# A head's TensorE order rearranged: scores, prediction and xs product together, output rows ahead of w_x, squares last, tile 3 in tile 2's bank

## The reference, cut to what matters

```python
# keys, values, queries of a head; chunk_loss = sum(mean((mlp(k) - v)**2) * lr)
grads = vmap(grad(chunk_loss))(mem_ws, keys, lr, values)     # for w0 and w1, by chunk
momentum = assoc_scan(mom_gate, -grads); updates = assoc_scan(1 - decay, momentum)
x    = einsum('bhncd,bhnde->bhnce', q, mem_w0 + updates[0])
vals = einsum('bhncd,bhnde->bhnce', silu(x), mem_w1 + updates[1])
vals = rmsnorm(vals) * (gamma + 1) * gate
out  = concat_heads(vals) @ w_combine
```

## Time and profile before

| | |
|---|---|
| median of 3 runs | 1191.07 us (1189.88 to 1191.84) |
| profiled execution | 1189.44 us, its span 1187.6 us |
| PE busy | 1100.7 us, 93% of the span |
| PE weight loads busy | 917.9 us, 77% |
| DVE, ACT, POOL busy | 720.1, 679.8, 561.9 us (61%, 57%, 47%) |
| mean granted TensorE clock | 0.965 |

### The profile page before, as it was taken

One profiled execution on the slowest core, in us unless ns is written; L12 is line 12 of the kernel. 1 busy time (PEld: TensorE's weight loads), 2 busy tenths in 40 slices (PEclk: granted clock), 3 DMA queues, 4 the chain that ended last, 5 costly groups with the idle time before them and its releaser, 6 DMA issues. The chain is left out here.

```text
span 1187.6 us, 20255 instructions
## 1 busy us (share of the span) xinstructions
PE 1100.7 (93%) x6649; PEld 917.9 (77%) x6650; DVE 720.1 (61%) x1892; ACT 679.8 (57%) x1369; POOL 561.9 (47%) x571
## 2 busy tenths in 40 slices
PE   4589869999999999999999899998999899999995
PEld 3356547788888888888888788887888788888884
DVE  4488856877655655655555455554555555556785
ACT  4666635566565565655555455554556455556663
POOL 3167753487764434444433343343434343344553
PEclk9888959999999999999999899999999999999998
DMA  9133330000300000000000000000000000002222
GB/s 209 38 89 90 89 115 1 1 21 21 98 24 1 2 16 10 10 10 18 9 10 7 20 8 10 8 9 19 8 8 9 19 8 10 3 5 77 88 88 72
DMA packets 57537, 40.32 MB, mean 34 GB/s; under 512 B 4595, under 2 KB 52061, under 8 KB 57310
## 3 DMA queue, kind: packets, MB, share of 16 engines
q1 hardware_dynamic: 53894, 32.10, 9.9%
q0 software_dynamic: 2304, 4.74, 1.2%
q10 hardware_dynamic: 1248, 2.23, 0.6%
HBM read 21.71 MB, written 15.50 MB: 31 GB/s over the span
## 5 line engine op out<-in xcount | busy, mean ns | idle before, releaser
L1105 DVE TENSOR_TENSOR p_sb<-bank,cf 128x512 f32<-128x512 f32 (+3 forms) x512 | 218.9, 483 | 1.1 <-PE bank L828 1.0
L1286 POOL TENSOR_TENSOR sq_rest<-sq,sq_high 128x450 f32<-128x450 f32 x64 | 67.2, 1050 | 247.1 <-ACT sq_high L995 247.1
L851 PE MATMUL bank<-p_sb,du_t 128*128 128x450 f32 (+3 forms) x512 | 131.1, 399 | 0.0
L851 PE MATMUL bank<-p_sb,err_t 128*128 128x450 f32 (+3 forms) x512 | 130.1, 397 | 0.0
L851 PEld LDWEIGHTS bank<-p_sb,err_t 128*128 128x128 f32 x512 | 85.0, 190 | 40.0 <-DVE p_sb L1105 16.9
L851 PEld LDWEIGHTS bank<-p_sb,du_t 128*128 128x128 f32 x512 | 82.0, 190 | 43.8 <-issue 29.8
L1138 DVE SCALAR_TENSOR_TENSOR acc<-bank,rg,acc 128x128 f32<-128x128 f32 x224 | 62.9, 344 | 84.6 <-POOL rg L1274 84.6
L1290 POOL TENSOR_TENSOR sq_low<-sq_rest,sq_mid 128x450 bf16<-128x450 f32 x64 | 66.6, 1041 | 100.1 <-ACT sq_mid L1012 99.9
L973 ACT ACTIVATE s_sb<-bank 128x512 f32<-128x512 f32 x64 | 38.3, 599 | 108.0 <-PE bank L828 108.0
L967 ACT ACTIVATE xs<-bank 128x450 f32<-128x450 f32 x64 | 35.1, 548 | 109.7 <-PE bank L851 108.5
L1174 DVE SCALAR_TENSOR_TENSOR du<-q_sb,bank 128x512 f32<-128x512 f32 x64 | 44.0, 688 | 87.5 <-PE bank L828 87.5
(11 more groups left out here) (304 smaller groups left out, 3193.0 us busy)
## 6 DMA issues: line engine op xcount, KB each, us to landing
x<-in_L_attn_inputs SPq DMA_DIRECT2D x16, 256.0 KB, 3.1
rows<-sorted_rows SPq DMA_DIRECT2D x40, 64.5 KB, 1.8
sorted_rows<-xl_all SPq DMA_DIRECT2D x1, 2064.0 KB, 14.7
x_rows<-x SPq DMA_DIRECT2D x8, 256.0 KB, 2.4
xn_rows<-xn SPq DMA_DIRECT2D x8, 256.0 KB, 2.4
xl_all<-xl SPq DMA_DIRECT2D x8, 256.0 KB, 3.4
ew<-in_L_ffn_w SPq DMA_DIRECT2D x8, 256.0 KB, 4.2
attn_out<-acc SPq DMA_DIRECT2D x7, 256.0 KB, 2.0
```

What stands on the lines that cost most here:

```text
L851: last = pe.matmul(out[:, P * i:QW], rows[:, i, :], p_sb[:, P_COL[i]:P_COL[i] + QW - P * i], start=False, stop=True, skip_group_check=True)
L1105: last = nc.vector.tensor_tensor(dst, src, w, ALU.mult)
L1286: nc.gpsimd.tensor_tensor(sq_rest[:], sq[:], sq_3[0][:], ALU.subtract).then_inc(g_rest, 1)
```

## The change: what it does

On PE the scores for s are parted: the tiles in halves (`NEAR`, 0 and 1) stay where they were, and the f32 ones (`FAR`, 2 and 3) come after the prediction and the xs product. Then follow the block's transpose (now into QA), the transposes of `err`, and only then the application to `err_t`. The scores for f are made in one go ahead of the transposes of `du`. The second expert layer and the output rows come ahead of the product with `w_x` and its application; the squares come last. Tile 3 lies in bank 6 beside tile 2. ACT makes `err_t` directly after `vals`, ahead of the squares. DVE weighs the near tiles, makes the first `q_sb`, and then weighs the far ones; the block's first DVE operation comes after the second `q_sb`.

The diff, cut to its core:

```diff
-SC_BANK = [4, 5, 6, 5]
-SC_COL = [0, 0, 0, 384]
-P_COL = [0, 512, 1024, 896]
-SC_ORDER = [0, 1, 3, 2]
+SC_BANK = [4, 5, 6, 6]
+SC_COL = [0, 0, 0, 256]
+P_COL = [0, 512, 896, 1152]
+NEAR, FAR = (0, 1), (2, 3)
...
-                        if i != 1:
+                        if i != 2:
                             last.then_inc(done, 1)
...
-                        scores(s_2[s[1] % 2], xs_2, s_sb[s[1] % 2][:, 2 * P:], xs, p_s1)
-                    if x is not None:
-                        r = s[1] % RING
-                        pe.wait_ge(m.s_rows[r], 16 * (turn(s) + 1))
-                        pe.wait_ge(a_xs, k + 1)
-                        pe.transpose(XB[:, 0:P], m.rows[r][:, 0:D], m.ident[:]).then_inc(p_t, 1)
+                        scores(s_2[s[1] % 2], xs_2, s_sb[s[1] % 2][:, 2 * P:], xs, p_s1, NEAR)
                     if f is not None:
                         pe.wait_ge(g_sl, n + 1)
                         product(EB[:], [w[:] for w in w1], [part[:] for part in s_2[h % 2]], start=False).then_inc(p_e, 1)
                     if s is not None:
                         pe.wait_ge(v_acc, k)
-                        pe.wait_ge(a_et, k + 1)
                         product(VB[:, 0:QW], [w[:] for w in w1], [part[:] for part in xs_2])
-                        apply(VB, err_t, v_p1, k).then_inc(p_v, 1)
+                        scores(s_2[s[1] % 2], xs_2, s_sb[s[1] % 2][:, 2 * P:], xs, p_s1, FAR)
                     if x is not None:
...
                         last.then_inc(p_et, 1)
+                    if s is not None:
+                        pe.wait_ge(a_et, k + 1)
+                        apply(VB, err_t, v_p1, k, NEAR + FAR).then_inc(p_v, 1)
...
-                        scores(yk, qa_2, yb, qa, p_s0, SC_ORDER[:-1])
+                        scores(yk, qa_2, yb, qa, p_s0, NEAR + FAR)
                         pe.wait_ge(v_du, n + 1)
                         for t in range(T):
                             last = pe.transpose(EB[:, t * P:t * P + P], du[:, t * P:t * P + P], m.ident[:])
                         last.then_inc(p_dt, 1)
-                        scores(yk, qa_2, yb, qa, p_s0, SC_ORDER[-1:])
-                        pe.wait_ge(a_et, n + 1)
-                        project(XB, m.w_x, f, SHIFT)
-                        pe.wait_ge(a_dt, n + 1)
-                        apply(XB, du_t, v_p0, n).then_inc(p_x, 1)
...
                             pe.matmul(VB[0:r, t * P:t * P + P], vals[:, t * P:t * P + r], m.w_out[:, s[1], :], start=True, stop=True)
+                    if f is not None:
+                        pe.wait_ge(a_et, n + 1)
+                        project(XB, m.w_x, f, SHIFT)
+                        pe.wait_ge(a_dt, n + 1)
+                        apply(XB, du_t, v_p0, n, NEAR + FAR).then_inc(p_x, 1)
+                    if s is not None:
                         pe.wait_ge(g_lo, k + 1)
```

More of the change, by code:

```diff
@@ L834, in project, with scores @@
                     return product(out[:, 0:width], [part[:, at[1], :] for part in w], y, stop=stop)
-                def scores(left_2, right_2, left, right, done, tiles=SC_ORDER):
+                def scores(left_2, right_2, left, right, done, tiles):
                     for i in tiles:
                         out = m.bank[SC_BANK[i]][:, SC_COL[i]:SC_COL[i] + QW - P * i]
-                        if i < 2:
+                        if i in NEAR:
                             last = product(out, [part[:, i * P:i * P + P] for part in left_2], [part[:, P * i:] for part in right_2])
@@ L843, in scores, with apply @@
                             last = pe.matmul(out, left[:, (i - 2) * P:(i - 1) * P], right[:, P * i:], start=True, stop=True)
-                        if i != 1:
+                        if i != 2:
                             last.then_inc(done, 1)
[L847 to L850, removed]
+                def apply(out, rows, made, n, tiles):
+                    for i in tiles:
+                        pe.wait_ge(made, SC_BANKS * n + min(i + 1, SC_BANKS))
                         last = pe.matmul(out[:, P * i:QW], rows[:, i, :], p_sb[:, P_COL[i]:P_COL[i] + QW - P * i],
@@ L882, in step @@
                         pe.wait_ge(v_acc, k)
[L883 removed]
                         product(VB[:, 0:QW], [w[:] for w in w1], [part[:] for part in xs_2])
[L885 removed]
+                        scores(s_2[s[1] % 2], xs_2, s_sb[s[1] % 2][:, 2 * P:], xs, p_s1, FAR)
                     if x is not None:
[L887 removed]
+                        r = s[1] % RING
+                        pe.wait_ge(m.s_rows[r], 16 * (turn(s) + 1))
                         pe.wait_ge(a_qa, n + 1)
[L889 to L891 removed]
+                        pe.transpose(QA[:, 0:P], m.rows[r][:, 0:D], m.ident[:]).then_inc(p_t, 1)
                     if f is not None:
@@ L897, in step @@
                         last.then_inc(p_et, 1)
+                    if s is not None:
+                        pe.wait_ge(a_et, k + 1)
+                        apply(VB, err_t, v_p1, k, NEAR + FAR).then_inc(p_v, 1)
+                    if x is not None:
+                        pe.wait_ge(v_xf, x + 1)
+                        for k4 in range(FB):
+                            last = pe.matmul(QA[:, k4 * P:k4 * P + P], w1s[:, k4 * P:k4 * P + P], xf, start=True, stop=True)
+                        last.then_inc(p_h, 1)
+                    if f is not None:
                         pe.wait_ge(v_el, n + 1)
@@ L991, in step @@
                         nc.scalar.copy(vals[:], VB[:, 0:QW]).then_inc(a_v, 1)
+                    if f is not None:
+                        act.wait_ge(p_et, n + 1)
+                        nc.scalar.copy(err_t[:].rearrange("p t d -> p (t d)"), XB[:]).then_inc(a_et, 1)
+                    if s is not None:
                         act.wait_ge(a_v, k + 1)
@@ L1095, in shifted, with weigh @@
                     nc.vector.tensor_copy(alpha_q[:], QA[:, 0:NT]).then_inc(v_shifted, 1)
-                def weigh(h, made, done, n):
-                    for i in SC_ORDER:
+                def weigh(h, made, done, n, tiles):
+                    for i in tiles:
                         ch = NC - 2 * i
@@ L1158, in step @@
                             nc.vector.tensor_tensor(yb[:], high[:, 2 * P:], low[:, 2 * P:], ALU.add).then_inc(v_y, 1)
+                        dve.wait_ge(a_th, n + 1)
+                        dve.wait_ge(a_s, n + 1)
+                        nc.vector.scalar_tensor_tensor(q_sb[:], U[:], 1.0, s_sb[h % 2][:], ALU.add, ALU.subtract).then_inc(v_q, 1)
+                    if s is not None:
+                        weigh(s[1], p_s1, v_p1, k, FAR)
+                    if f is not None:
                         if h == 0:
```

29 lines of the change are left out of this document (13 added, 16 removed).

## The result

The changed kernel takes 1214.53 us (median of 4 runs, 1213.51 to 1215.03), the kernel before beside it 1191.45 (1189.88 to 1193.96): ratio 1.0182, 95% interval 1.0163 to 1.0201. It is slower by 23 us; the forecast was 1216 with 1206 to 1226. The profiled execution's span is 1213.3 us (before 1187.6). From the first product of w_u to the end it takes 1036.9 us where it took 1015.4, and 176.4 where it took 172.1 in the part ahead of it, which the change doesn't touch.

What follows compares the result with a forecast made beforehand. PE, busy throughout each head, was taken as the bound, with `s_low` gating the prediction. Plain heads +13.1 and expert heads +14.0, less 2.5 hidden, gave +24.6 us: 1216 us, range 1206 to 1226.

Steps and rivals of the forecast that it cites:

- The far scores and `s_low`: Front of the head: PE waits for POOL's `s_low` once far scores move behind the prediction; +0.62 plain, +0.40 expert.
- The -0.26 through the early `rs`: Expert heads: scatter over by then, so `rs` is not held up and the prediction starts at 3.44, not 3.70.
- The size of what moved: Work that came before the prediction and now comes after it: 0.55 us in plain, 0.66 in expert heads.
- xs later, +0.07: Plain head, ACT: `s_sb` starts 0.74 after the mark, 0.07 later than now; nothing added in an expert head.
- Squares behind the application, -0.05: Head's end: the second application is followed by a square's short load, saving 0.05 us per head.
- `err_low` and the relus, 0: Waits for DVE's `err_low` (covered by about 0.1 plain, 0.5 expert) and ACT's relus (0 to 0.3, taken as 0).
- Expert heads, +0.35 in 40: Each of 40 expert heads grows by 0.40 - 0.05 = +0.35 us, together 14.0.
- 2.5 us hidden in the longer heads: In the dozen longer heads something else is late and hides part of the stall: at most 5.4, taken as 2.5.
- No change: Rival: POOL reaches `s_low` early enough that PE loses only about 0.1 a head; 1191 us, chance 0.04.
- faster: Rival: crossings between halves and f32 carry the price and `s_low` does not hold the prediction; 1185 us, chance 0.05.
- Slower still: Rival: covers of `err_low` and the relus fail, 0.2 more in each of 63 heads; 1229 us, chance 0.06.
- The rule on the shared port: Head's front: `xs_low` and POOL's `rs` exclude each other; `xs_low` waits, near scores end at 3.06, sum the same.

Runs made afterwards that it cites:

- e8: The changed kernel unaltered, run and profiled again: 1215.89 us, ratio 1.0174 to the kernel before.
- e9: The kernel before, unaltered, run and profiled once more: 1194.76 us, one run.
- e2: The changed kernel with the prediction's product that needs `s_low` put last of its three: 1192.25 us, ratio 0.9974 to the kernel before.
- e5: e2 with the first xs product moved ahead of the product that needs `s_low`: 1184.3 us, ratio 0.9914 to the kernel before.
- e3: The changed kernel with PE's front of the step in the order of before, changed tail kept: 1206.1 us, ratio 1.0077 to the kernel before.
- e7: The kernel before with only the prediction's `s_low` product put last: 1190.48 us, ratio 0.9973 to the kernel before.
- e4: The changed kernel with w_x and its application directly behind the transposes of `du` on PE again, changed front kept: 1244.67 us, ratio 1.0411 to before.
- e1: The changed kernel with the far scores for s ahead of the prediction again: 1201.15 us, ratio 1.0048 to the kernel before.
- e6: e5 with first-batch counts and shifts behind the application to `du_t`, and last-batch gate product between the squares' subtractions: 1178.47 us, ratio 0.9869 to before.

## Why the prediction was right, point by point

The differences of the first pair by batch are, in us: batch 0 +7.6, batch 1 +4.4, batch 2 +3.0, batches 3 to 6 in the loop +0.2, -1.4, -0.2 and 0.0, batch 7 with the end +8.0. They add up to the 21.5 (and to 20.3 in e8 less e9, with +6.7, +5.9, +3.0, -1.8 for the loop and +6.5). The forecast was +24.6. Its cause is right, but that its sum is near is in good part luck: the 40 expert heads were to cost 14.0 and cost 1.5, the plain heads with the edges were to cost 10.6 and cost 20.0.

- *The far scores and `s_low`: right.* `s_low` starts the prediction in both kinds of head, at 3.45 after the mark (forecast 3.51 and 3.44). The -0.26 through the early `rs` came out as forecast in the expert heads of the loop. In batch 2 it is only 0.15, since `s_low` ended 3.41 to 3.44 after the mark there before, and not at 3.54. e2 and e5 fill the hole and give 0.43 and 0.5 to 0.6 a head back: shown.
- *The size of what moved: 0.05 too large.* Far scores now cost 350.73 - 350.23 = 0.50, and with the block's transpose 0.61, not 0.55 and 0.66. It is the order of the two tiles. Before, the two passes of 66 columns came first, and the pass of 194 behind them took 0.22 to the next start; now the two of 194 come first and take 0.16 each. What follows the tiles is not it: in the expert head of the earlier trace rows a transpose follows them, and they take 0.55 even so. The prediction had the 0.05 that passes of 66 cost when a long load follows them, and said that all of them but those ahead of the squares keep one behind them. The far scores didn't: the transposes follow them now, and the first takes 0.11 to the next start like the others. That is read from rows, no run isolates it.
- *xs later, +0.07: did not come.* `s_sb` starts 0.67 after the mark, as in the earlier trace rows. From `xs_high` to `s_sb` it is 346.14 - 345.62 = 0.52 and not the 0.57 + 0.03 I took: ACT's next operation starts before the modelled end of the one before. The start-to-start step was the thing to read.
- *Squares behind the application, -0.05: right.* 359.00 - 357.20 = 1.80 from the application's start to the next product, where it was 1.85.
- *A plain head:* 0.50 - 0.05 = +0.45, as measured, for +0.57 forecast.
- *`err_low` and the relus, 0: right for the changed kernel.* That they cost nothing hangs on the order of the front: e3 takes the early transposes of `err` away and the relus cost 0.4 in an expert head at once.
- *Expert heads, +0.35 in 40: this term failed.* In batch 2 the number holds (15.70 to 16.07, +0.37), with less gained at `rs` and less lost in what moved than the term had. In the 32 heads of the loop the steady ones lost only 0.14, and the turns won: the first two heads of a turn went from 20.3 and 17.4 to 20.0 and 17.0 (why, stays open). So the loop's batches changed by -1.5 in all instead of +11.2. What the term had at nothing without saying so are the loop's own waits. Two waits of 0.07 to 0.08 stand in the steady loop heads of before and not of after. One precedes the first w_u product: 0.109 from the last square, now 0.032. The other lies in the first pass of the application to `du_t`: 0.448 to the second pass, now 0.378. With -0.26 + 0.61 - 0.05 = +0.30 for the order they give +0.15. The first goes with the tail of the step: squares to w_u is 0.10 to 0.11 in the loop's heads of before, e9, e7 and e4, all with the tail of before, and 0.03 in e3, which has the front of before and the changed tail, and in e1, e2, e5 and e6. The second is gone in e3 too (0.377; e7 0.446), while in e4 the wait for `du_t` hides it. Which move within the tail does it no run tells apart. My expectation of e3 put both waits down to register loads; no row of a trace shows one.
- *2.5 us hidden in the longer heads: wrong in sign at the edges.* Batches 0, 1 and 7 lost 20.0 us where the term had 23 x 0.57 less the hidden part, 10.6. Three causes are visible. In the last two heads of batch 0 and the first of batch 1 POOL has one more product in its queue, ahead of `rs`, here in the last of batch 0:

```profile
284.92 0.99 POOL L1260 DMA_INDIRECT sorted_rows<-xl_all,place  x1 [0.17 <-issue]
285.94 0.81 POOL L1264 TENSOR_TENSOR ew<-lr_th,starts 128x256 f32<-128x256 f32 x1
286.71 1.44 POOL L1277 TENSOR_TENSOR rs<-ms,neg_half 128x4 f32<-128x4 f32 x1
...
288.38 1.26 POOL L1268 TENSOR_TENSOR s_low<-s_sb,s_high 128x512 fp32r<-128x512 f32 x1
```

  The squares come last now, so this chain begins later against the next head's mark, `s_low` ends at 289.64, and PE waits 1.09 by its row instead of 0.34 (before it did not wait there at all); the head takes 14.93 where it took 13.74. In the fifth head the shift products wait for DVE with three jobs behind them (e6 gives 1.28 back). In batch 7:

```profile
1158.66 1.15 POOL L1297 TENSOR_TENSOR sq_low<-sq_rest,sq_mid 128x450 bf16<-128x450 f32 x1 [0.68 <-ACT sq_mid L1015]
1159.77 1.26 POOL L1313 TENSOR_TENSOR ew<-ew 128x512 f32<-128x512 f32 x1
1161.97 1.49 POOL L1277 TENSOR_TENSOR rs<-ms,neg_half 128x4 f32<-128x4 f32 x1 [0.94 <-DVE ms L1122]
```

  The gate product comes behind the later `sq_low`, DVE's sum waits for it ahead of `ms`, and `rs` and `s_low` follow: 14.63 instead of 13.70 for four heads, of which e6 gives back 0.52. The first head of batch 1 lost 1.25 (waits of 1.09, 0.42 and 0.77 for `s_low`, `p_sb` and `err_low` where one of 1.38 for `err_low` stood), and e6 does not give it back. The program's end was 3.6 us longer in the first pair and 2.0 in e8 less e9, with a granted clock of 0.53 in a stretch of 3.6 us in the first; how much of it is the change's stays open.
- *The rivals.* "No change" and "faster" needed PE to run on at `s_low`'s place; it didn't, and e2 has the same crossings at 0.43 less. "Slower still" did not come here; its part on the relus came in e3.
- *The rule on the shared port.* In the earlier trace rows `rs` took 1.35 beside an `xs_low` that had started first. Now `rs` begins first (345.65 to 346.69), and `xs_low` runs inside it (346.22, 0.63) without waiting, at its old length; `rs` takes 1.04, as when alone. The Trainium skill ("SBUF — State Buffer", "SBUF: two separate sides") would have `xs_low` blocked to the end of `rs`; this row does not agree. The near scores end 2.83 after the mark and not at 3.06. But the rule is not idle in this kernel: where the larger `ew` (128x256) runs on POOL first, from 285.94 to 286.75 in the rows above, `xs_low` takes 0.91 and not 0.63:

```profile
286.33 0.91 DVE L1128 TENSOR_TENSOR xs_low<-xs,xs_high 128x450 fp32r<-128x450 f32 x1 [0.66 <-ACT xs_high L971]
```

  And where `xs_low` came first, `rs` took less than a wait to the end of `xs_low` would make it: in the earlier trace rows that would be 345.22 + 0.61 + 1.05 - 345.39 = 1.49, and it took 1.35. The prediction's "the trace agrees" was too strong.

## What to carry to other kernels

Find for each wait the work that stands in front of it, and price a reordering by the cover that it takes away: here 0.5 us of independent matmuls moved past one semaphore cost 0.45 us in a plain head, and two or three products that did not need the late half (0.20 to 0.23 each) put in the same place gave as much or more back. Then ask how long the engine stands still at the place, for the same edit was worth 0.43 us a head where the hole was 0.61 and 0.03 where it was 0.05. Ask also which wait is next behind the one you cover: in e1 it was `err`, and in the loop's heads of e7 `p_sb`. Price the heads at the edges and in the hardware loop by their own rows, since a step's gain in the middle says nothing of them.

## What the runs showed of the hardware that I had not expected

- A DVE operation on two SBUF inputs (`xs_low`) and a POOL operation ran side by side without loss when the POOL one was `rs` (128x4) and began first, 1.04 and 0.63 us. Where the DVE one began first, `rs` took 1.32 to 1.49, and where both began within 0.03 us mostly 1.49 to 1.53 (two cases of 1.04). In the changed kernel `xs_low` took 0.91 to 0.93 where POOL's `ew` (128x256) had begun first.
- The delay from the end of POOL's `s_low` to PE's first product behind the wait was 0.15 to 0.17 us in 56 heads of the kernel before and in 60 of the changed one.
- Two executions of an untouched stretch differed by 4 us (172.1 and 175.9 in the same kernel), as much as the whole edit of e7 is worth; only pieces compared by their own length told what an edit did. The granted clock does not explain it: it was 0.85 both in the 172.1 us of before and in the 176.1 us of e8.
